# Windowed attention and a Fourier mixer on one core: x loaded two turns ahead, y stored in halves, a two-turn TensorE loop, and the q/k products between the halves of the second layer

## The reference

```python
# layer 0: shifted 4x4 window attention, 64 channels, 4 heads, then an MLP; x is (8, 256, 256, 64)
qn, kn = q / max(|q|, 1e-12), k / max(|k|, 1e-12)      # per head of 16
attn = softmax(qn @ kn.T * scale + bias)               # 16 positions of a window
a = (attn @ v) @ proj_w.T + proj_b
x = x + layernorm(a, norm1_g, norm1_b)
h = gelu(x @ fc1_w.T + fc1_b) @ fc2_w.T + fc2_b        # 64 -> 256 -> 64
x = x + layernorm(h, norm2_g, norm2_b)
# layer 1: per channel, moving average plus a 128-mode Fourier mix over the row index
trend = moving_average(x, 25)
x = trend + irfft(einsum(rfft(x - trend)[:128], w_real + 1j * w_imag))
```

## Time and the profile before

| | |
|---|---|
| median of 3 runs | 8832.92 us (8820.32 to 8860.32) |
| profiled execution | 8844.13 us |
| its span, first to last instruction | 8842.3 us |
| mean granted TensorE clock | 0.905 of full speed |
| busy: PE, DVE, ACT, POOL | 80%, 72%, 63%, 57% of the span |
| long stage, first transpose to the last one | 269 to 7534 us |

### The profile page before, as it was taken

The page is one execution under the profiler, slowest core; times in us unless marked ns, Lnnn a source line. Parts: engine busy times, 40 slices in busy tenths (PEclk is TensorE's granted clock), DMA queues, the critical chain, the costliest instruction groups (busy, mean ns, idle before and its releaser), DMA issues.

```text
span 8842.3 us, 274685 instructions
## 1 busy us (share of the span) xinstructions
PE 7043.9 (80%) x105272; PEld 4365.9 (49%) x105272; DVE 6343.8 (72%) x8543; ACT 5588.4 (63%) x7004; POOL 5069.9 (57%) x4616
## 2 busy tenths in 40 slices
PE   8777888787878888877787887878887778778786
PEld 5544444444444444444444444444444444467675
DVE  1777888887888888877888888888887788422221
ACT  1566777776777777776777777777776677522221
POOL 0566676666666767666766666666766667200000
PEclk9988999998899989988999999999998899888888
DMA  3344444444444444444444444444444444599999
GB/s 100 105 109 110 113 113 107 113 113 109 111 112 109 115 111 115 113 110 110 112 108 112 113 113 112 113 113 112 114 107 110 108 113 113 167 351 335 352 335 334
DMA packets 1408944, 1247.65 MB, mean 141 GB/s; under 512 B 657809, under 2 KB 1067793, under 8 KB 1404051
## 3 DMA queue, kind: packets, MB, share of 16 engines
q1 hardware_dynamic: 1403588, 1101.36, 47.3%
q10 hardware_dynamic: 4608, 134.22, 3.6%
HBM read 412.97 MB, written 285.21 MB: 79 GB/s over the span
## 4 chain that ended last, share of the span: by engine, by line
PE 33%; DVE 19%; DMA 16%; issue 14%; SPq 12%; ACT 5%; DVEq 1%; ACTq 0%; POOL 0%; POOLq 0%
PE ps L615 9%; DMA arena<-in_x 7%; PE ps L578 5%; DMA arena<-arena 5%; SPq L358 4%; DVE arena L844 4%; DMA out<-arena 3%; PE ps L590 3%; PE ps L546 3%; SPq L333 3%; PE ps L562 3%; PE ps L534 2%; SPq L363 2%; DVE arena L867 2%; DVE arena L856 2%
## 5 line engine op out<-in xcount | busy, mean ns | idle before, releaser
L578 PE MATMUL ps<-arena 64*128 64x512 f32 x4096 | 1251.4, 737 | 400.5 <-issue 200.4
L985 POOL TENSOR_TENSOR arena<-arena 128x512 f32<-128x512 f32 x1024 | 1072.4, 1068 | 316.4 <-PE ps L534 315.9
L978 POOL TENSOR_TENSOR arena<-arena 128x1024 f32<-128x1024 f32 x512 | 980.4, 1915 | 273.5 <-DVE arena L823 273.5
L615 PE MATMUL ps<-rows,amat 128*128 128x256 f32 x4096 | 912.1, 386 | 242.8 <-ACT arena L734 195.6
L590 PE MATMUL ps<-arena 128*64 128x512 f32 x4096 | 1088.0, 655 | 7.5 <-ACT arena L713 5.6
L713 ACT ACTIVATE arena<-ps,arena 128x1024 f32<-128x1024 f32 x1024 | 1081.6, 1112 | 0.0
L578 PEld LDWEIGHTS ps<-arena 64*128 64x128 f32 x4096 | 437.4, 221 | 1175.8 <-issue 1010.2
L615 PEld LDWEIGHTS ps<-rows,amat 128*128 128x128 f32 x4096 | 793.8, 194 | 362.4 <-ACT arena L734 199.7
L1017 POOL TENSOR_TENSOR arena<-arena 128x512 f32<-128x512 f32 x512 | 542.2, 1059 | 740.8 <-DVE arena L876 740.8
L823 DVE TENSOR_TENSOR arena<-ps,arena 128x1024 f32<-128x1024 f32 x512 | 611.7, 1195 | 473.2 <-PE ps L485 473.2
L562 PE MATMUL ps<-arena 64*64 64x512 f32 x2048 | 589.7, 648 | 424.7 <-DMA arena<-arena 424.1
(11 more groups left out here) (94 smaller groups left out, 15398.6 us busy)
## 6 DMA issues: line engine op xcount, KB each, us to landing
rows<-arena SPq DMA_DIRECT2D x4096, 64.0 KB, 2.0
arena<-in_x SPq DMA_DIRECT2D x1024, 128.0 KB, 2.5
arena<-arena SPq DMA_DIRECT2D x512, 256.0 KB, 2.8
arena<-arena SPq DMA_DIRECT2D x1024, 128.0 KB, 2.3
y<-ystripe SPq DMA_DIRECT2D x256, 512.0 KB, 5.4
amat<-mix SPq DMA_DIRECT2D x512, 256.0 KB, 3.4
rows<-y SPq DMA_DIRECT2D x512, 256.0 KB, 4.1
out<-arena ACTq DMA_DIRECT2D x32, 4096.0 KB, 27.3
```

The costliest lines, as they stand in the source:

```text
L578: ins = mm(M[:, a, :], w1[a * C:a * C + C, kk * P:(kk + 1) * P], x1T[ring(g, 4)][a * C:a * C + C, :], start=True, stop=True, tile_position ...
L615: ins = mm(ps[:, j, k * T:(k + 1) * T], amat[j][:, r * T + k * P:r * T + (k + 1) * P], xch[j][:, r * T:(r + 1) * T], start=(r == 0), stop= ...
L978: tt(sq, q, q, ALU.mult).then_inc(squared, 1)
L985: tt(vexp.rearrange("p s h e d -> p (s h) e d")[:, :, e, :], vb[ring(g, 4)].rearrange("p (n d) -> p n d", d=HD), par[:, e:e + 1].unsqueeze ...
```

## The change

Five edits, all in the long stage:

1. **x in two buffers.** `xin` becomes a pair with a semaphore each; `load_x` of group s waits for the transpose of group s-2, and it stands ahead of the SP operations of turn s-1, where it stood behind them.
2. **y in halves.** `store_y` runs in every second turn, with two DMAs of 8 rows (256 KB) each.
3. **A fifth kind of copy.** `x1T` has two buffers in place of four, and a new DMA (`copy_x1`, 256 KB) per turn copies x1 to one of four buffers `x1r`, which POOL's `add2` reads. `add1` on DVE waits in addition for `first_layer` 1 and for that copy, both of two groups before. The hidden layer `hT` moves into memory that the other stages use.
4. **PE's loop** has a body of two turns in place of four.
5. **Order.** PE: `project_qk` stands between the two halves of `second_layer`. ACT: `square1` between the two `gelu`. SP: `swap_halves` ahead of `spread_p`.

```diff
-        xin = carve(4 * P).rearrange("p (s n) -> p s n", s=4)
+        xin = [carve(4 * P).rearrange("p (s n) -> p s n", s=4) for _ in range(2)]
...
-        x1T = [carve(512) for _ in range(4)]
+        x1T, x1r = [carve(512) for _ in range(2)], [carve(512) for _ in range(4)]
...
+        mats = sb("mats", NB * 512)
+        amat = [mats[:, i * 512:(i + 1) * 512] for i in range(NB)]
+        hT = [mats[:, i * 1024:(i + 1) * 1024].rearrange("p (a n) -> p a n", a=2) for i in (1, 2)]
...
+        def need_slot(eng, s, g, n, loads=1):
+
+            if there(g):
+                r, per = ring(g, n), 16 * loads // n
+                eng.wait_ge(s[r], g.base * per + (g.off - r + n) * per)
...
             def load_x(s, q, g):
                 if there(g):
-                    need(sp, xT_ps, before(g))
+                    need(sp, xT_ps, before(g, 2))
...
+            def copy_x1(g):
+                if there(g):
+                    need(sp, x1_sb, g)
+                    sp.dma_start(x1r[ring(g, 4)], x1T[ring(g, 2)]).then_inc(x1r_in[ring(g, 4)], 16)
...
             def store_y(s, h):
                 need(sp, y_sb, h)
+                u = ring(h, 8) // 2
                 for a in range(2):
                     sp.dma_start(
-                        yr[bass.ds(s * ROWS, ROWS), :, a * HALF:(a + 1) * HALF].rearrange("r c n -> c r n"),
-                        ystripe[ring(h, 8) // GPS][a * C:(a + 1) * C]).then_inc(y_out[ring(h, 8) // GPS], 16)
+                        yr[bass.ds(s * ROWS + u % 2 * 8, 8), :, a * HALF:(a + 1) * HALF].rearrange("r c n -> c r n"),
+                        ystripe[u // 2][a * C:(a + 1) * C, u % 2 * 8:u % 2 * 8 + 8, :]).then_inc(y_out[u], 16)

             def turn(b, k):
                 copy_x(Group(b, k - 1))
+                copy_x1(Group(b, k - 8))
+                swap_halves(Group(b, k - 7))
                 spread_p(Group(b, k - 5))
-                swap_halves(Group(b, k - 7))
                 spread_k(Group(b, k - 3))
...
                 for k in range(8):
                     load_x(d * 2 + k // GPS, k % GPS, Group(d * 8, k))
-                    turn(d * 8, k)
-                    if k % GPS == 0:
-                        store_y(d * 2 + (k // GPS - 4), Group(d * 8, k - 16 + GPS - 1))
+                    turn(d * 8, k - 1)
+                    if k % 2 == 0:
+                        store_y(d * 2 + (k - 14) // GPS, Group(d * 8, k - 13))
...
                 second_layer(i9, 0, fc2a_ps)
+                project_qk(i1)
                 second_layer(i9, 1, fc2b_ps)
-                project_qk(i1)
                 project_v(i1)
                 variances(i7, i9)

-            over_groups(pe, step, 4)
+            over_groups(pe, step, 2)
...
                 keep_o(i6)
                 gelu(i9, 0, MA, fc1a_ps, fc2a_ps, gelu0)
+                square1(i7)
                 gelu(i9, 1, MB, fc1b_ps, fc2b_ps, gelu1)
-                square1(i7)
                 keep_x(i0)
...
                         need(dve, xr_in, g, 16)
                         need(dve, y_sb, before(g, 4))
-                        stt(x1T[ring(g, 4)], D1, g1, xr8[ring(g, 8)], ALU.mult, ALU.add).then_inc(x1_sb, 1)
+                        need(dve, fc1b_ps, before(g, 2))
+                        need_slot(dve, x1r_in, before(g, 2), 4)
+                        stt(x1T[ring(g, 2)], D1, g1, xr8[ring(g, 8)], ALU.mult, ALU.add).then_inc(x1_sb, 1)
...
                 def add2(g):
                     if there(g):
                         need(pool, yg_sb, g)
+                        need_slot(pool, x1r_in, g, 4)
```

More of the change, by code:

```diff
@@ L157, in swin_then_fourier @@
         sq1, sq1x, sq2, dn2, yg = (carve(512) for _ in range(5))
-        x1T = [carve(512) for _ in range(4)]
+        x1T, x1r = [carve(512) for _ in range(2)], [carve(512) for _ in range(4)]
         l12, r12 = (carve(1024).rearrange("p (k n) -> p k n", k=2) for _ in range(2))
-        hT = [carve(1024).rearrange("p (a n) -> p a n", a=2) for _ in range(2)]
         ystripe = [sb(f"ystripe{i}", ROWS * HALF)[:, :].rearrange("p (r n) -> p r n", r=ROWS)
@@ L167, in swin_then_fourier @@
         vri = [sb(f"vri{i}", 512) for i in range(2)]
-        amat = [sb(f"amat{i}", 512) for i in range(NB)]
+        mats = sb("mats", NB * 512)
+        amat = [mats[:, i * 512:(i + 1) * 512] for i in range(NB)]
+        hT = [mats[:, i * 1024:(i + 1) * 1024].rearrange("p (a n) -> p a n", a=2) for i in (1, 2)]
         rows = sb("rows", NB * 512)
@@ L188, in swin_then_fourier @@
         made_id, wts = sem("made_id"), sem("wts")
-        x_in, y_out = sem("x_in"), [sem("y_out0"), sem("y_out1")]
+        x_in, y_out = [sem("x_in0"), sem("x_in1")], [sem(f"y_out{i}") for i in range(4)]
         xT_ps, qk_ps, v_ps2, S_ps, pv_ps, proj_ps = (
             sem(n + "_ps") for n in ("xT", "qk", "vproj", "S", "pv", "proj"))
+        x1r_in = [sem(f"x1r_in{i}") for i in range(4)]
         xr_in, kTx_in, pTx_in, xTc_sb = sem("xr_in"), sem("kTx_in"), sem("pTx_in"), sem("xTc_sb")
@@ L374, in _ @@
                 load_x(i // GPS, i % GPS, Group(i, 0))
-                turn(i, 0)
+                turn(i, -1)
+                if i % 2 == 0 and i >= 14:
+                    store_y((i - 14) // GPS, Group(i - 13, 0))
             with sp.Fori(2, NS // 2) as d:
@@ L378, in _ @@
                     load_x(d * 2 + k // GPS, k % GPS, Group(d * 8, k))
-                    turn(d * 8, k)
-                    if k % GPS == 0:
-                        store_y(d * 2 + (k // GPS - 4), Group(d * 8, k - 16 + GPS - 1))
[L382 to L387, removed]
+                    turn(d * 8, k - 1)
+                    if k % 2 == 0:
+                        store_y(d * 2 + (k - 14) // GPS, Group(d * 8, k - 13))
+            for i in range(G, G + 14):
+                turn(i, -1)
+                if i % 2 == 0:
+                    store_y((i - 14) // GPS, Group(i - 13, 0))
+            for i in range(4):
+                sp.wait_ge(y_out[i], 8 * NS)
             for j in range(2):
@@ L471, in turn_x @@
                     if there(g):
-                        need(pe, x_in, g, 16 * 2)
+                        need_slot(pe, x_in, g, 2, 2)
                         after(pe, (oT_sb, i6), (xT_sb, before(g)))
@@ L735, in put @@
                   ps[:, j, :].unsqueeze(2), ACT.Copy).then_inc(o_act, 1)
-            for i in range(2):
-                act.wait_ge(y_out[i], 16 * NS)
+            for i in range(4):
+                act.wait_ge(y_out[i], 8 * NS)
             for b in range(BL1):
@@ L807, in mix_step @@
                     dve.wait_ge(m_out[j], c2 * 16)
-                tt(amat[j][:, :], ps[:, j, :], avgm[:, :], ALU.add).then_inc(m_sb, 1)
+                tt(amat[j], ps[:, j, :], avgm[:, :], ALU.add).then_inc(m_sb, 1)
             for j in range(2):
@@ L945, in put @@
                                 ps[:, j, :].unsqueeze(2)).then_inc(o_dve, 1)
-            for i in range(2):
-                dve.wait_ge(y_out[i], 16 * NS)
+            for i in range(4):
+                dve.wait_ge(y_out[i], 8 * NS)
             for b in range(BL1):
@@ L1027, in add2 @@
                         need(pool, yg_sb, g)
+                        need_slot(pool, x1r_in, g, 4)
                         r = ring(g, 8)
-                        if r % GPS == 0:
+                        if r % 2 == 0:
                             if there(before(g, 8)):
-                                pool.wait_ge(y_out[r // GPS], g.base * 4 + (g.off - r) * 4)
+                                pool.wait_ge(y_out[r // 2], g.base * 4 + (g.off - r) * 4)
                         v = "p (x r j e) -> p x r e j"
                         tt(ystripe[r // GPS][:, r % GPS * WIN:(r % GPS + 1) * WIN, :].rearrange("p r (x e j) -> p x r e j", x=N, j=WIN),
-                           yg.rearrange(v, r=WIN, j=WIN, e=2), x1T[ring(g, 4)].rearrange(v, r=WIN, j=WIN, e=2),
+                           yg.rearrange(v, r=WIN, j=WIN, e=2), x1r[ring(g, 4)].rearrange(v, r=WIN, j=WIN, e=2),
                            ALU.add).then_inc(y_sb, 1)
```

10 lines of the change are left out of this document (5 added, 5 removed).

## The result

The changed kernel takes 8030.33 us (median of 4 runs, 8027.61 to 8037.56), the kernel before 8826.62 in the same comparison: a ratio of 0.9096, 95% interval 0.9066 to 0.9125. The forecast was 7860 in a range of 7600 to 8200.

What follows compares the result with a forecast made beforehand. TensorE's late x and long loop branches were taken as bounds, with VectorE beneath. 57.22 - 4.25 - 3.6 = 49.4 us per pass; 124 x 7.8 = 970 us off 8844.13 gives 7874, so 7860 against the median run, range 7600 to 8200.

Steps and rivals of the forecast that it cites:

- x two turns ahead: TensorE's wait for x behind the stores: an earlier load removes it, worth 4.25 us per four turns.
- The loop of two turns: TensorE's loop branch: a halved body always finds its code in place, saving 3.6 us per four turns.
- two-page rule: TensorE's loop branch: a taken branch outside two 16 KiB pages always fetches; by it the pass would be 61.3 us.
- the rival built on that mechanism: TensorE's loop branch: a body over two blocks always misses, two long branches per pass, 9340 us; chance 0.04.
- The copy of x1, its waits and SP's load: DMA, `add1` and SP: the extra copy fits at 60% DMA share; waits cost 0 to 0.2 us per turn.
- The rival of late swaps: SP or DMA queues: swaps land late in the two turns of four with a store, 8510 us; chance 0.10.
- The order: Reordering on PE, ACT and SP: waits and order together -2.4 to +0.8 us per pass, taken as 0.
- the cover: ScalarE's 1.35 us wait for POOL before `exponent` hides later `square1`; without it 1.2 us per turn lie open.
- What lies beneath both is VectorE: Beneath the x and branch stalls VectorE sets the pace, 12.35 us per turn, range 11.9 to 12.95.
- x and code together: The x stall's 4.25 us and the long branches' 3.6 us per pass of four turns, summed as the gain.

Runs made afterwards that it cites:

- the early waits: The changed kernel with the waits of `add1` placed ahead of `normed1` on VectorE: 8035.78 us, ratio 0.91.
- the old orders: The changed kernel with the three order moves on PE, ACT and SP undone: 8050.25 us, ratio 0.912.

## Why the prediction was right, and where it was off

**x two turns ahead: right, sized too small.** The load lands in time in every turn. Its worth was 4.25 us per four turns in the forecast and 665 / 124 = 5.4 in the changed kernel.

**The loop of two turns: right in kind, sized too large.** All branches are short and no block is fetched, and with a body of four turns 57 of 95 passes fetch one or none. So the two-page rule of the Trainium skill ("Runtime: NRT & Kernel Launch", section Instruction fetch mechanics) doesn't hold for TensorE here; the rival built on that mechanism fell. The forecast took 3.6 us per four turns, six long branches in ten at 5.95. The price came from a difference of two means divided by 0.4, with 59.6 us from only four passes; the long passes of the kernel before take 58.81, and sorted one by one they give 4.0 us each, 0.6 x 4.0 = 2.4 per four turns. In the sum this is the term that was mis-sized: with 2.4 it gives 57.22 - 4.25 - 2.4 = 50.6 us per pass and 8844 - 124 x 6.6 - 11 = 8010. With the rest of the change in place a loop of four gives up 221 / 124 = 1.8, four in ten at 4.7.

**The copy of x1, its waits and SP's load: right.** `add1`'s gap grew from 0.19 us to 0.29 in the timeline above, inside the 0 to 0.2 allowed, and costs nothing, as the early waits show. The DMA share is 0.55, where 0.60 was expected. The rival of late swaps didn't come.

**The order: right, and worth nothing here.** `square1` waits 435.7 / 394 = 1.1 us for `project`, 1.2 were forecast; the cover held. PE's wait for swaps went, and the old orders gave the same time within 20 us.

**The turn beneath the stalls: this is the mechanism that was off.** "What lies beneath both is VectorE" took VectorE alone as the bound, and 12.35 was put near the middle between the 11.71 of rows 6 and the 12.95 of rows 2. The mean turn is 12.71 us, 1.4 us more per pass, 180 us in all, which is about the miss. Beneath the stalls lies a loop of VectorE and GpSimd through a port, 12.51 us. The 11.71 of the earlier trace rows doesn't measure the turn: it begins with a `normed1` that started 1.03 us late, behind ScalarE, and so leaves that wait out. By the reciprocals the same turn takes 12.83 us:

```profile
4255.87 0.35 DVE L889 RECIPROCAL arena<-arena 128x32 f32<-128x32 f32 x1
...
4262.71 0.58 DVE L850 TENSOR_SCALAR arena<-arena 128x64 f32<-128x64 f32 x1
...
4268.70 0.35 DVE L889 RECIPROCAL arena<-arena 128x32 f32<-128x32 f32 x1
```

GpSimd had got ahead meanwhile, and so the clamp found the port sooner, 0.58 us. Two further terms missed in opposite directions and in part cancelled, which is luck: x and code together were put at 7.85 us per pass and are 5.4 + 1.8 = 7.2, each measured with the rest of the change in place. The pass gained 57.22 - 4 x 12.71 = 6.4.

## What to carry to other kernels

An operation whose duration varies from turn to turn with the same shape is waiting inside its own duration; compare its end with what the other engines end at that moment. If a VectorE operation waits so for GpSimd, it is best placed where GpSimd is idle: here one line moved two places was worth 423 us, over half as much as the whole change. And an interval that begins with an operation held up by a stall comes out too short. The floor beneath a stall should be taken from a loop of releases, with a mark on that loop: the reciprocal had 12.50 us in the trace of the kernel before already, the start of `normed1` 11.71.

## What the runs showed that I had not expected

- The clamp of 128 x 64 elements takes 184 ns while GpSimd is idle and 1039 ns on average at its old place, also with two SBUF inputs (1059 ns); all 394 end 49 to 58 ns after GpSimd's `add2`. The wait goes the other way too: GpSimd's `expand_v` takes 1.22 us in place of 1.04 where `gain2` is ahead of it.
- A TensorE loop whose code fits is left at 215 ns per branch, 196 times of 196. The same kernel with twice the body has branches up to 5183 ns, and how often depends on more than the size of the body: 64 of 105 in one kernel, 39 of 96 in another.
- TensorE's clock fell for one `first_layer` (3.68 us for 1.99) in about every fifth turn although the engine was 88% busy. The mean of the steady part was 0.97, and 1.00 in the kernel with the clamp moved, an edit on VectorE alone.
